# ScalarE scales the gathered rows chunk by chunk, VectorE the sums of a group, and VectorE splits a batch at the end of its step

## The reference

```python
def _ngcf_conv(x, W1, W2, src, dst, n_nodes):
    deg_out = clip(segment_sum(ones, src), 1.0)
    deg_in = clip(segment_sum(ones, dst), 1.0)
    norm = rsqrt(deg_out[src] * deg_in[dst])
    h_src, h_dst = x[src], x[dst]
    msg = (h_src @ W1 + h_src * h_dst @ W2) * norm[:, None]
    return x @ W1 + segment_sum(msg, dst)

h = relu(_ngcf_conv(x, W1_1, W2_1, src, dst, n))
h = _ngcf_conv(h, W1_2, W2_2, src, dst, n)
out = layernorm(x + h)
```

## Time and profile before

| | |
|---|---|
| three runs | 1139.75, 1142.33, 1142.66 us; median 1142.33 |
| profiled execution, its own time | 1141.05 us |
| its span | 1139.3 us |
| busy, share of the span | PE 72%, DVE 87%, ACT 65%, POOL 73% |
| chain that ended last | POOL 33%, issue 11% (all of it in layer two's gathers) |

### The profile page before, as it was taken

One profiled execution on the slowest core, in us unless ns is written; L12 is line 12 of the kernel. 1 busy time (PEld: TensorE's weight loads), 2 busy tenths in 40 slices (PEclk: granted clock), 3 DMA queues, 4 the chain that ended last, 5 costly groups with the idle time before them and its releaser, 6 DMA issues. The chain is left out here.

```text
span 1139.3 us, 33680 instructions
## 1 busy us (share of the span) xinstructions
PE 821.3 (72%) x13104; PEld 754.9 (66%) x13104; DVE 990.9 (87%) x2382; ACT 736.3 (65%) x2733; POOL 833.9 (73%) x811
## 2 busy tenths in 40 slices
PE   1676567888888877777773677777777877778774
PEld 0565356787787867677773676676667776667764
DVE  8999888999999977777775479989998999899997
ACT  2200235888888987777772367667766787677775
POOL 7388777777777777777764777777777777777771
PEclk9999877988989998878887779989998889898997
DMA  9976312322222322222233233444444334443333
GB/s 208 191 226 260 114 27 51 82 69 66 80 66 67 81 67 67 54 67 68 68 67 91 51 76 83 97 94 103 92 90 92 86 89 89 94 93 86 88 82 66
DMA packets 148545, 105.05 MB, mean 92 GB/s; under 512 B 115752, under 2 KB 128744, under 8 KB 147820
## 3 DMA queue, kind: packets, MB, share of 16 engines
q1 hardware_dynamic: 123032, 71.17, 22.8%
q0 software_dynamic: 25216, 32.50, 15.7%
q10 hardware_dynamic: 212, 0.42, 0.1%
HBM read 58.92 MB, written 45.11 MB: 91 GB/s over the span
## 5 line engine op out<-in xcount | busy, mean ns | idle before, releaser
L819 POOL DMA_INDIRECT c_rows<-table,k_row_i x394 | 383.7, 974 | 136.6 <-issue 119.8
L819 POOL DMA_INDIRECT k_rows<-table,k_row_i x346 | 348.3, 1007 | 105.5 <-issue 105.2
L878 PE MATMUL c_out<-k_wcat,c_uvt 128*128 128x64 f32 x1516 | 216.6, 304 | 71.2 <-ACT c_uvt L960 68.9
L878 PEld LDWEIGHTS c_out<-k_wcat,c_uvt 128*128 128x128 f32 x1516 | 210.7, 220 | 86.1 <-ACT c_uvt L960 55.7
L951 ACT ACTIVATE c_sum<-c_sum,k_xh 128x64 f32<-128x64 f32 x762 | 164.4, 307 | 156.4 <-DVE c_sum L1170 155.9
L1111 DVE TENSOR_SCALAR c_sel<-k_place,k_grid 128x512 bf16<-128x512 f16 (+1 forms) x788 | 245.3, 379 | 0.0
L852 PE MATMUL c_sum<-c_rows,c_sel 128*128 128x64 bf16 x4701 | 169.8, 202 | 46.6 <-DVE c_rows L1121 45.9
L852 PEld LDWEIGHTS c_sum<-c_rows,c_sel 128*128 128x128 bf16 x4701 | 166.5, 104 | 50.5 <-issue 48.9
L938 ACT ACTIVATE c_own<-k_xh 128x64 f32<-128x64 f32 x762 | 195.2, 387 | 0.0
L852 PE MATMUL c_sum<-c_yr,c_sel 128*128 128x64 bf16 x1567 | 179.0, 206 | 1.8 <-DVE c_lo L1141 1.8
L852 PE MATMUL c_sum<-c_rest,c_sel 128*128 128x64 bf16 x1567 | 178.0, 207 | 0.0
(11 more groups left out here) (209 smaller groups left out, 1230.8 us busy)
## 6 DMA issues: line engine op xcount, KB each, us to landing
table<-c_y SPq DMA_DIRECT2D x47, 384.0 KB
out<-c_y SPq DMA_DIRECT2D x47, 256.0 KB, 2.6
c_res<-in_x SPq DMA_DIRECT2D x46, 256.0 KB
c_rows<-table,k_row_i POOLq DMA_INDIRECT x394
k_rows<-table,k_row_i POOLq DMA_INDIRECT x346
table<-k_xh SPq DMA_DIRECT2D x1, 3640.0 KB
table<-k_xh SPq DMA_DIRECT2D x2, 1820.0 KB
table<-k_xh SPq DMA_DIRECT2D x1, 3575.0 KB
```

Of the source, the lines that this page charges most:

```text
L819: nc.gpsimd.indirect_dma_start(out=rows[:, b % RING, i], out_offset=None, in_=tables[l], in_offset=bass.IndirectOffsetOnAxis(ap=k.row_i[:, ...
L878: last = nc.tensor.matmul(out_bank(g)[:, n, :], uvt[:, g % 2, n, :], weights, start=True, stop=True)
```

## The change

In layer one, four things move; layer two keeps its order.

- The scaling of gathered rows goes from VectorE, one operation a batch, to ScalarE: `scale_rows(b)`, one operation a chunk, 8 a batch, at the head of ScalarE's step. It waits for the rows and, for batches 1 to 5, for a new semaphore `norms_known`.
- The scaling of the sums goes from ScalarE, one operation a tile, to VectorE, one operation a group (`scale(g)`, which the tail already had).
- On VectorE, `scale` and `products` come before `select`, and `cut(s)` after it, with the counting behind; in the tail likewise.
- Of the eight picks for a batch, four now stand among the selections, one between the rest and the low part and three behind it.

```diff
+            def scale_rows(b):
+                landed(act, b)
+                done(act, summed, b - 1)
+                if b > AHEAD - 1 and b < EARLY:
+                    act.wait_ge(norms_known, b - AHEAD + 1)
+                for i in range(BATCH[b]):
+                    last = A(yr[:, b % 2, i], rows[:, b % RING, i, 0:D], ACT.Copy, scale=rows[:, b % RING, i, D:ROW])
+                last.then_inc(rows_scaled, 1)
...
-                for g in ended(s - 1):
-                    scale(g)
+                if l == 0:
+                    scale_rows(s)
+                else:
+                    for g in ended(s - 1):
+                        scale(g)
...
-            scale(g0)
             if l == 0:
+                scale_rows(b0)
+                scale_rows(b1)
                 relu(g0 - 1)
+                scale_rows(b2)
                 turned_back(g0)
...
-                step(V.scalar_tensor_tensor(rows[:, b, :, D], q, 1.5, r, ALU.add, ALU.mult))
+                V.scalar_tensor_tensor(rows[:, b, :, D], q, 1.5, r, ALU.add, ALU.mult).then_inc(norms_known, 1)
...
                     if b - 1 in LOOKUPS and i % 2 == 1:
-                        pick(LOOKUPS[b - 1], 4 + i // 2)
+                        pick(LOOKUPS[b - 1], i // 2)
...
-                pick_next(0)
-                landed(dve, b)
+                dve.wait_ge(rows_scaled, b + 1)
                 done(dve, summed, b - 1)
-                V.tensor_tensor(yr[:, j, 0:n], rows[:, b % RING, 0:n, 0:D], rows[:, b % RING, 0:n, D:ROW].to_broadcast([P, n, D]), ALU.mult).then_inc(rows_scaled, 1)
-                pick_next(1)
-                dve.wait_ge(rows_scaled, b + 1)
...
             for s in STEPS:
-                split_up(s)
+                if l == 1:
+                    split_up(s)
                 for g in ended(s - 1):
                     join(g)
                 if l == 0:
                     for g in ended(s - 3):
                         rests(g)
+                    for g in ended(s - 1):
+                        scale(g)
+                        products(g)
                 select(s + 1)
+                if l == 0:
+                    split_up(s)
...
-            split_up(b0)
+            if l == 1:
+                split_up(b0)
             join(g0)
             if l == 0:
                 rests(g0 - 2)
-            select(b1)
-            if l == 1:
+                scale(g0)
+            else:
+                select(b1)
                 deviate(g0 - 3)
             products(g0)
+            if l == 0:
+                select(b1)
+                split_up(b0)
             split_up(b1)
```

More of the change, by code:

```diff
@@ L700, in layer @@
             rows_scaled, rest_made, hidden_made = (sem(n) for n in ("rows_scaled", "rest_made", "hidden_made"))
-            flat_made, high_made = sem("flat_made"), sem("high_made")
+            flat_made, high_made, norms_known = sem("flat_made"), sem("high_made"), sem("norms_known")
         else:
@@ L1125, in cut @@
                 n, j = BATCH[b], b % 2
-                def pick_next(i):
-                    if b in LOOKUPS:
-                        pick(LOOKUPS[b], i)
-                pick_next(0)
-                landed(dve, b)
+                dve.wait_ge(rows_scaled, b + 1)
                 done(dve, summed, b - 1)
-                V.tensor_tensor(yr[:, j, 0:n], rows[:, b % RING, 0:n, 0:D], rows[:, b % RING, 0:n, D:ROW].to_broadcast([P, n, D]), ALU.mult).then_inc(rows_scaled, 1)
-                pick_next(1)
-                dve.wait_ge(rows_scaled, b + 1)
                 high = yr[:, j, 0:n].rearrange("p c d -> p (c d)")
                 V.tensor_tensor(rest[:, j, 0:n].rearrange("p c d -> p (c d)"), high, top(high), ALU.subtract).then_inc(rest_made, 1)
-                pick_next(2)
+                if b in LOOKUPS:
+                    pick(LOOKUPS[b], 4)
                 dve.wait_ge(rest_made, b + 1)
@@ L1141, in cut @@
                 V.tensor_tensor(lo[:, j, 0:n].rearrange("p c d -> p (c d)"), low, top(low), ALU.subtract).then_inc(split, 1)
-                pick_next(3)
+                if b in LOOKUPS:
+                    for i in range(5, 8):
+                        pick(LOOKUPS[b], i)
             def rests(g):
@@ L1309, in vector @@
                         deviate(g)
-                for g in ended(s - 1):
-                    products(g)
+                    for g in ended(s - 1):
+                        products(g)
                 if l == 0 and s == 10:
```

## The result

The changed kernel takes **1277.84 us** in the median of four runs (1272.23 to 1279.42), the kernel before 1141.26 us in four: a ratio of 1.118, 95% interval 1.115 to 1.121. The profiled execution has a span of 1277.7 us. So the direction was right, and the time lies 16 us above the range given; it is the time of rival B, 1278.

The account below looks back on a forecast made before the run. Layer one, gather-bound before, was to become a serial VectorE-TensorE loop: early steps +15, 42 steps +77.0, tail -2.6, together 89 us on 1141.05, so 1230 us; 8-in-10 range 1197 to 1262.

Parts of the forecast that it names:

- rival B: Layer one's loop in series with TensorE on the low clock throughout: 12.14 us a step, 1278 us; chance 0.08.
- the early steps: Steps 0 to 4 of layer one, with look-ups: more picks ahead of the cut, +15 us (5 to 20).
- the 42 steps: Layer one, cut of batch 5 to that of batch 47: 11.01 us each, 462.4 us, +77.0 us.
- the tail: Layer one from the cut of batch 47 to the last operation: 22 us instead of 24.7, -2.6 us.
- item 2's matmul term: The 96 matmuls of a layer-one batch, in series with VectorE: 3.58 us, at the mean clock of before.
- item 2: Layer one: cut behind the selections puts VectorE and TensorE in series, 11.01 us a step (10.48 to 12.14).
- Item 1: Layer one's row scaling on ScalarE: ready 4.0 us after the join begins, needed at 5.0, so hidden.
- The gathers' waiting on buffers: GpSimd in layer one waits for ScalarE's scaling to free buffers: 25 to 30 us in all, costing nothing.
- Rival C: Layer one stays gather-bound; fewer two-SBUF-input VectorE operations slow gathers less: gain up to 21 us, 1120 us; chance 0.06.
- Rival D: Gathers stay layer one's bound, held by as many VectorE operations as before: no difference, 1141 us; chance 0.05.

Follow-up runs that it names:

- The filler runs: The changed kernel with 72 or 24 extra unread matmuls per step on TensorE ahead of the adding-up: 1223.04 us with 72, 1224.86 us with 24.

## Why the prediction was right or wrong

The parts of the prediction's sum, measured by its own points: the early steps +17.8 us (the rest of batch 5 at 215.87 against a cut at 198.09) where it said +15; the 42 steps 499.1 us where it said 462.4; the tail 28.5 us where it said 22; and layer two 3.2 us more where it said nothing (from its first gather to the end of the span 530.9 us, against 527.7 before, where that gather stands at 611.61). 17.8 + 113.7 + 3.8 + 3.2 = 138.4 us, the difference of the spans.

*What failed: item 2's matmul term.* "For 11.01 I take the mean clock of before, since TensorE's work in a step is as before". The work was, but not where the idling lay. And the mean of before was a mixture. Of its batches 6 to 47, 27 took 3.05 us and 15 took 4.0 to 5.2. In the trace of before each of the 15 has a pause of TensorE of 2.1 to 3.1 us between its adding-up and the one ahead, and of the 27 all but two have none longer than 1.6. One of the 15, the pause and then the adding-up (PE busy and count, PEld, DVE, ACT, POOL, clock, DMA, GB/s):

```profile
351.10:353.20 2.10, 0.03 (x1) 0.00 (x0) 2.07 (x5) 2.07 (x7) 1.49 (x3) 1.00 0.11 20
355.10:359.70 4.60, 4.60 (x100) 4.60 (x100) 3.80 (x7) 4.46 (x18) 3.69 (x4) 0.63 0.19 30
```

In the change every step has such a pause, 2.9 us, right ahead of the adding-up, and the granted clock is at its lower level when the adding-up begins. So the rows for the slow price were there. The adding-up took 4.84 us and not 3.58, 1.26 us in each of 42 steps, 53 us. The filler runs show this as cause: with the clock held, the adding-up is at 3.04 us and the kernel gets 55 to 60 us back. The other parts of the loop were 0.34 us too long in my sum: 6.83 for 7.05 (the selections took 2.24, not 2.50, a step) and a hand-over of 0.15 for 0.27. 11.01 + 1.26 - 0.34 is 11.93, and 499.1/42 is 11.88. The range had the same fault: item 2 names 12.14 us a step as the slow end, which is 1278 us, and the range stops at 1262.

*What held.* The mechanism: the join's and the matmuls' waits of 45 steps each, and the kernel with the late cut alone, at 1.112. ScalarE off the path: no wait for scaled rows ahead of the tail, and no gain from scaling ahead. Item 1 has VectorE need the scaled rows at 5.0 us; its own list of item 2 adds up to 5.63 ahead of the rest, and measured are 5.39 (413.14 to 418.53), so the 1.0 us to spare was 1.5. The gathers' waiting on buffers costs nothing, though it came to 92 us and not 25 to 30, since the loop was slower. The early term was 3 us short.

*Rival B* had the right number by the right words ("TensorE idles about 3 us in one piece in each step"), and I gave it 0.08. Its own argument was stronger than the one against it, which was a mean over steps with another pattern. Its 4.71 us was a low-clock row; the steps here took 4.41 and 5.28 by turns. That its 1278 us is met to the microsecond is luck: its loop of 509.9 us is 10.8 too long, and the early steps, the tail and layer two, which it has as in the sum, came out 12.4 us longer together. Nor was the clock low throughout, as it says, but in all of one adding-up and most of the next.

*Rival C* was wrong for the change and right as a mechanism: the gathers themselves gained 16.6 us in the change (348.3 to 331.7), and 8.8 with the loop open. But the gain is not a price of the operation taken out. With rest and low part in each step the gathers took 331.5 to 339.5 us in eight kernels; with the scaling of rows beside them on VectorE 343.8 (the late cut alone) and 348.3 (before). What counts is how many gathers start inside such an operation, and how early in it. Two rows of before, of the batch of the earlier trace rows:

```profile
223.60 0.69 DVE L1141 TENSOR_TENSOR c_lo<-c_rest 128x512 bf16<-128x512 f32 x1
...
223.96 1.15 POOL L819 DMA_INDIRECT k_rows<-table,k_row_i  x1 [0.30 <-issue]
```

The gather starts 0.36 us into the low part and ends 0.82 us behind its end; that of the earlier trace rows also ends 0.82 us behind the end of the scaling (222.84). In layer one of before 82 gathers start well inside such an operation (0.05 us in or later, and not in its last 0.06): all end 0.76 to 0.86 us behind its end, are 1.19 us long in the mean, and make 19.8 of the 21.3 us of excess. The 40 that start ahead of one that they overlap, or in its first 0.04 us, take 0.96 us. With scaling ahead and the cut at the head 44 gathers are held. The Trainium skill ("SBUF — State Buffer", Who interferes with whom) infers that a two-input tensor operation leaves descriptor writing alone, which gives no hold; here the measurement decides against that. The same section also says that such an operation contends with GpSimd instructions that read SBUF, and that the order of issue decides who is blocked; these rows agree with that (the gather reads its row numbers, `k_row_i`, from SBUF), and the prediction left this rule out. Rival D, for which the gathers stay the bound and are held as often as before, is out by the total and by the gathers' time.

*The tail* was wrong in sign, 6.5 us over the 22. The walk through VectorE's list had left out that ScalarE's scaling of the last two chunks stands behind a relu that waits for TensorE; this is the 4.8 us wait above, behind a relu that had waited 7.1 us for TensorE. The matmuls of batch 47, at 4.52 us instead of 3.58, are another 0.9. Mending the tail in the kernel with the cut at the head took it from 30.6 to 22.7 us; in the change itself it was not tried. Of the 3.2 us in layer two 2.6 are in the gathers' own time (386.3 us against 383.7). Layer two is the same code in all ten kernels, and in their traces it takes 523.8 to 530.9 us, with gathers of 379.8 to 386.6: so this term is within what layer two varies by itself. Why it varies is open.

The expectations of two runs missed as well: with the cut at the head or ahead of the selections I had counted 8.6 to 10.2 and 9.7 us, and asked only whether that is under the gathers' 10.1. But VectorE must for the first half of the layer be faster than the gathers, since it starts some 50 us behind them: before, its steps took 9.2 us in the mean (385.4/42). And the adding-up was slower there too, 3.93 us per 96 with the cut at the head and 4.23 with it ahead of the selections.

## What to carry to other kernels

When an operation is moved to the end of an engine's step, list what the next step's first operation waits for: if that comes out of the moved one through another engine, the two engines no longer overlap, whatever either's busy share says. Price such a loop with the matmuls at the clock that they will have behind the new pause, not at the mean of the old pattern: look in the old trace for the runs of matmuls that stand behind such a pause, and take theirs. And an operation given to another engine takes that engine's place in line with it: the same eight operations, one place further ahead in ScalarE's list, were worth 50 us once the loop was open.

## What the runs showed of the hardware

The granted clock fell from 1.00 to 0.50 within a 2.9 us pause of TensorE and stayed for the 5.3 us of matmuls behind it; 24 matmuls without use, some 0.8 us a step, kept it up throughout 18 of 35 batches and made the kernel 50 to 60 us faster. The length of the pause doesn't settle it: with pauses of at most 1.5 us 36 of 43 batches of another kernel were slow as well. A matmul with the start flag on columns 448 to 511 of a PSUM bank disturbed sums kept in columns 0 to 391 of the same bank; without the flag it left them alone. The Trainium skill ("PSUM — Partial Sum Buffer", The four PSUM rules) says that the flag acts on a whole 2 KB bank, and these two runs agree. And a gather from GpSimd that starts inside a VectorE operation that reads two tensors from SBUF is held until 0.82 us behind that operation's end, 1.19 us long in the mean instead of 0.95 (82 gathers of before); one that starts just ahead of it isn't. Taking one such operation out of each step saved 8.8 to 16.8 us of 348.3, by how the gathers fell.
